# Dividing attention outputs instead of probabilities, and causal scores of two heads in two row tiles

## The reference

```python
# layer 1, full attention with head mixing (head_w sums the six heads' q), then a norm per head
s = q_mixed @ k.T * hd ** -0.5          # 256 x 256 a head
p = softmax(s)
p = (p - mean(p)) / sqrt(var(p) + 1e-5) * gamma + beta      # over the whole 256 x 256 map of a head
y = p @ v
# layers 2 and 3, causal attention
p = softmax(where(causal, q @ k.T * hd ** -0.5, -inf))
y = x + (p @ v) @ w_proj + b_proj
```

## Time and profile before

| | |
|---|---|
| median of 3 runs | 978.55 us (974.76 to 978.98) |
| profiled execution | 974.61 us, of which the span of the trace is 972.6 us |
| busy in the span | PE 83%, DVE 79%, ACT 65%, POOL 20% |
| layer 1 loop | 107 to 329 us |
| causal loop of layer 2 | about 393 to 532 us |
| causal loop of layer 3 | about 655 to 796 us |

### The profile page before, as it was taken

The page is one execution under the profiler, slowest core; times in us unless marked ns, Lnnn a source line. Parts: engine busy times, 40 slices in busy tenths (PEclk is TensorE's granted clock), DMA queues, the critical chain, the costliest instruction groups (busy, mean ns, idle before and its releaser), DMA issues.

```text
span 972.6 us, 19124 instructions
## 1 busy us (share of the span) xinstructions
PE 808.0 (83%) x5550; PEld 630.5 (65%) x5550; DVE 772.7 (79%) x2166; ACT 632.9 (65%) x1931; POOL 192.6 (20%) x234
## 2 busy tenths in 40 slices
PE   0876698889988755899999486559999997999997
PEld 0762576667766653678887356438778877677775
DVE  7327799999999835699999869938999994688886
ACT  0211587777877513689888564248889874688885
POOL 9001423443234110000000000010000010134344
PEclk9997899999999967799999798779999995799999
DMA  5000000000000091466666200035666650313130
GB/s 184 1 0 1 1 1 0 0 0 0 0 0 0 10 121 28 76 93 97 90 87 83 31 1 1 0 62 83 84 97 96 88 75 0 69 41 82 41 82 17
DMA packets 54355, 44.30 MB, mean 46 GB/s; under 512 B 28592, under 2 KB 42544, under 8 KB 54192
## 3 DMA queue, kind: packets, MB, share of 16 engines
q1 hardware_dynamic: 53872, 42.30, 27.9%
q0 software_dynamic: 448, 1.57, 0.6%
HBM read 12.33 MB, written 3.21 MB: 16 GB/s over the span
## 4 chain that ended last, share of the span: by engine, by line
PE 44%; DVE 12%; DMA 3%; issue 1%; ACT 1%; SPq 1%; POOL 0%; POOLq 0%; DVEq 0%; ACTq 0%
PE ps L839 7%; PE ps L850 6%; PE ps L720 6%; PE ps L624 6%; PE ps L670 5%; PE ps L661 3%; PE ps L626 3%; DVE chst L910 2%; DMA qk<-lo 2%; DVE on L929 2%; PE ps L551 1%; PE ps L634 1%; PE ps L635 1%; PE ps L647 1%; PE ps L826 1%
## 5 line engine op out<-in xcount | busy, mean ns | idle before, releaser
L419 ACT ACTIVATE ee<-ps,nmax 128x128 f32<-128x128 f32 (+1 forms) x588 | 249.5, 443 | 11.7 <-DVE nmax L990 9.9
L1031 DVE TENSOR_SCALAR ee<-ee,rrec 128x128 f32<-128x128 f32 (+1 forms) x588 | 174.8, 360 | 5.2
L720 PE MATMUL ps<-w,ee 128*128 128x128 f32 x960 | 137.0, 279 | 19.9 <-DVE ee L1031 19.9
L406 ACT ACTIVATE big<-ps 128x384 f32<-128x384 f32 (+1 forms) x224 | 113.5, 538 | 40.0 <-PE ps L720 39.4
L720 PEld LDWEIGHTS ps<-w,ee 128*128 128x128 f32 x960 | 103.9, 141 | 45.4 <-DVE ee L1031 35.6
L419 ACT ACTIVATION_READ_ACCUMULATOR ee<-ps,nmax 128x1 f32 x588 | 124.2, 211 | 0.0
L990 DVE TENSOR_REDUCE nmax<-ps 128x2 f32<-128x256 f32 x200 | 101.1, 545 | 18.0 <-PE ps L626 18.0
L624 PE MATMUL ps<-qk 128*128 128x128 f32 (+1 forms) x400 | 103.7, 348 | 13.4 <-DMA qk<-lo 10.8
L296 POOL TENSOR_TENSOR big<-qs,w 96x256 f32<-96x256 f32 x108 | 78.8, 761 | 144.4 <-ACT qs L429 144.4
L1234 DVE TENSOR_TENSOR hhl<-ee,hhl 128x512 fp32r<-128x512 f32 x96 | 81.7, 858 | 27.9 <-ACT hhl L525 26.2
L624 PEld LDWEIGHTS ps<-qk 128*128 128x128 f32 x400 | 79.8, 207 | 31.7 <-issue 17.9
(11 more groups left out here) (224 smaller groups left out, 1365.5 us busy)
## 6 DMA issues: line engine op xcount, KB each, us to landing
qk<-hi SPq DMA_DIRECT2D x36, 192.0 KB, 3.7
qk<-hi SPq DMA_DIRECT2D x72, 96.0 KB, 3.8
qk<-lo SPq DMA_DIRECT2D x36, 192.0 KB, 4.8
qk<-lo SPq DMA_DIRECT2D x72, 96.0 KB, 4.6
big<-moe_gate SPq DMA_DIRECT2D x8, 768.0 KB, 6.9
w<-w_in SPq DMA_DIRECT2D x1, 1831.5 KB, 12.9
xc<-x_in SPq DMA_DIRECT2D x4, 384.0 KB, 5.7
l_mix<-on SPq DMA_DIRECT2D x8, 192.0 KB, 6.6
```

The costliest lines, as they stand in the source:

```text
L406: nc.scalar.activation(et[:, h, 0:w], ps[:, 4 + hh, 0:w], ACT.Copy).then_inc(own(l, f"et{hh}"), 1)
L419: last = nc.scalar.activation(ee[:, ke, hh, qc, 0:w], src, ACT.Exp, bias=nmax[:, kp, hh, qc:qc + 1], accum_out=rsum[:, kp, hh, qc:qc + 1])
L720: last = nc.tensor.transpose(ps[:, 4 + hh, b * P:(b + 1) * P], ee[:, u, hh, qc, tc * P:(tc + 1) * P], ident)
L1031: last = V.tensor_scalar(v, v, rrec[:, kp, hh, qc:qc + 1], None, ALU.mult)
```

## The change

Four things, which come together:

1. Probabilities are no longer normalised. `vh` has a one in column 16 of each head's 32, so that `weigh_values` gives the row sums as a 17th output row of each head. `outputs` transposes to tokens by channels in all layers, and the new `normalise_outputs` (DVE) takes the reciprocal of 12 sums a token and multiplies. The row sums of `exps` on ACT go, and so do the reciprocals and the four multiplications of each unit on DVE. `transpose` waits for the exponentials.
2. In layer 1 the sum of squares comes from `bn_stats` of the exponentials (four of 256 columns a unit), put together after the loop by six DVE instructions of 192 or 384 columns.
3. In the causal layers, after `outputs` (moved from u = 1 to u = 0) and `normalise_outputs` (u = 1), the result is transposed back (`outputs_back`, PE, u = 1), copied by ACT (`outputs_by_channel`, first thing in u = 2), multiplied with an unsplit projection (`project_outputs`, PE, u = 2) and added (`add_outputs`, DVE, moved to u = 2). DVE does both `et` copies of u = 1, where ACT did both.
4. The two heads of a causal unit lie in rows 0 to 63 and 64 to 127 of `qk`, so each score matmul uses 64 rows. One mask matmul of 2 x 128 columns a head takes the place of two of 128. `stack` issues twelve DMAs of 48 partitions where it issued six of 96.

Besides, POOL's split of the expert weights (`w1hl`) moves from the end of layer 3 to the end of layer 1.

```diff
-STK = 16 * 6
+STK = 16 * 12
-        qk = sb("qk", [P, 2, NH, 2, N], F32R)
+        qk = sb("qk", [P, 2, NH // 2, 2, N], F32R)
...
                         for t, a0, a1 in moves:
-                            sp.dma_start(qk[t * HD:(t + 1) * HD, par, :, a0:a1, :].bitcast(F32),
-                                         part[:, a0:a1, :].bitcast(F32)).then_inc(own(l, "stacked"), 16)
+                            for hh in range(2):
+                                r0 = hh * 4 * HD + t * HD
+                                sp.dma_start(qk[r0:r0 + HD, par, :, a0:a1, :].bitcast(F32),
+                                             part[hh * (C // 2):(hh + 1) * (C // 2), a0:a1, :].bitcast(F32)).then_inc(own(l, "stacked"), 16)
...
-                    last = nc.scalar.activation(ee[:, ke, hh, qc, 0:w], src, ACT.Exp, bias=nmax[:, kp, hh, qc:qc + 1],
-                                                    accum_out=rsum[:, kp, hh, qc:qc + 1])
+                        last = nc.scalar.activation(ee[:, ke, hh, qc, 0:w], src, ACT.Exp, bias=nmax[:, kp, hh, qc:qc + 1])
...
+            def outputs_by_channel(l, i):
+                act.wait_ge(*upto(l, "oc_ps", i + 2))
+                nc.scalar.activation(oc[0:C, :], ps[0:C, 6, 0:N], ACT.Copy).then_inc(own(l, "oc"), 1)
...
+                        if l > 1 and u == 2:
+                            outputs_by_channel(l, i - 1)
                         exps(l, k + 1, (j + 1) % 2, (u + 1) % 3)
...
-                            h = 2 * u + hh
-                            mm(ps[:, 2 * kp + hh, qc * N:qc * N + w], qk[:, par, h, 0, qc * P:(qc + 1) * P], qk[:, par, h, 1, 0:w],
-                               start=True, stop=False)
-                            last = mm(ps[:, 2 * kp + hh, qc * N + qc * P:qc * N + (qc + 1) * P], identb[:, :], maskb[:, :], start=False, stop=True)
+                            r0 = hh * 4 * HD
+                            mm(ps[:, 2 * kp + hh, qc * N:qc * N + w], qk[r0:r0 + 4 * HD, par, u, 0, qc * P:(qc + 1) * P],
+                               qk[r0:r0 + 4 * HD, par, u, 1, 0:w], start=(qc == 0), stop=False)
+                    for hh in range(2):
+                        diag = ps[:, 2 * kp + hh, :].rearrange("p (b t) -> p b t", t=P)[:, 0::3, :]
+                        last = mm(diag, identb[:, :], mid_dim(maskb[:, :], 1, TPI), start=False, stop=True)
...
+            def outputs_back(l, i):
+                pe.wait_ge(*upto(l, "on", i + 2))
+                for q in range(TPI):
+                    last = nc.tensor.transpose(ps[0:C, 6, q * P:(q + 1) * P], ob[:, q, :], ident)
+                last.then_inc(own(l, "oc_ps"), 1)
+
+            def project_outputs(l, i):
+                pe.wait_ge(*upto(l, "oc", i + 2))
+                for q in range(TPI):
+                    last = mm(ps[:, 6, q * C:(q + 1) * C], oc[0:ONE + 1, q * P:(q + 1) * P], wa(f"l{l}_p", ONE + 1), start=True, stop=True)
                 last.then_inc(own(l, "out_ps"), 1)
...
+                        if l > 1 and u == 2:
+                            project_outputs(l, i - 1)
                         for hh in range(2):
-                            pe.wait_ge(*upto(l, "norm", 2 * k + (hh + 1)))
+                            pe.wait_ge(*upto(l, "exp", 2 * k + (hh + 1)))
...
                         if u == 0:
                             project_qk(l, i + 2, par)
+                            if l > 1:
+                                outputs(l, i - 1)
                         if u == 1:
-                            outputs(l, i - 1)
+                            if l == 1:
+                                outputs(l, i - 1)
+                            else:
+                                outputs_back(l, i - 1)
                             parts_ready(l, i + 2)
                             project_v(l, i + 1, npar)
...
+            def normalise_outputs(l, i):
+                dve.wait_ge(*upto(l, "oq", i + 2))
+                src = ps[:, 6, 0:4 * C].rearrange("p (q h d) -> p q h d", q=TPI, d=2 * HD)
...
+                V.reciprocal(rec, src[:, :, :, HD]).then_inc(own(l, "orec"), 1)
+                dve.wait_ge(*upto(l, "orec", i + 2))
+                for q in range(TPI):
...
+                    last = V.tensor_tensor(dst.rearrange("p (h d) -> p h d", d=HD), src[:, q, :, 0:HD], last_dim(rec[:, q, :], HD), ALU.mult)
+                last.then_inc(own(l, "on" if l > 1 else "added"), 1)
...
                         maxima(l, k + 2, j % 2)
-                        if l > 1 and u != 1:
+                        if l > 1 and u == 2:
+                            add_outputs(l, i - 1)
+                        if l > 1:
                             w = len(blocks(l)) * P
-                            dve.wait_ge(*upto(l, "tr", TR0 + 2 * k + 1))
-                            V.tensor_copy(et[:, 2 * u, 0:w], ps[:, 4, 0:w]).then_inc(own(l, "et0"), 1)
+                            for hh in range(2 if u == 1 else 1):
+                                dve.wait_ge(*upto(l, "tr", TR0 + 2 * k + hh + 1))
+                                V.tensor_copy(et[:, 2 * u + hh, 0:w], ps[:, 4 + hh, 0:w]).then_inc(own(l, f"et{hh}"), 1)
                         if l == 1:
-                            dve.wait_ge(sg("l1_norm"), 2 * k + 2)
-                            dve.wait_ge(sg("l1_ssq"), TR0 + k)
-                            for hh in range(1 if u == 2 else 2):
...
+                            dve.wait_ge(sg("l1_exp"), 2 * k + 2)
+                            for hh in range(2):
+                                for q in range(TPI):
+                                    last = V.bn_stats(est[:, par, q, 2 * u + hh, :], ee[:, u, hh, q, :])
+                            last.then_inc(sg("l1_est"), 1)
...
-                        normalise(l, k + 1, (j + 1) % 2, (u + 1) % 3)
                         if u == 0:
                             keys(l, i + 2)
                         if u == 1:
-                            add_outputs(l, i - 1)
+                            normalise_outputs(l, i - 1)
                             values(l, i + 1, npar)
```

More of the change, by code:

```diff
@@ L143, in hybrid_kernel @@
         junk = sb("junk", [P, N])
[L144 to L146 removed]
+        w1hl = sb("w1hl", [P, 2, NE * HID], F32R)
+        est = sb("est", [P, 2, TPI, NH, 6])
+        esta = sb("esta", [P, B, TPI, NH, 6])
         ssqa = sb("ssqa", [P, B, NH])
@@ L336, in _ @@
                     nc.gpsimd.tensor_tensor(w1hl[:, 1, :], wa("f3_w1"), w1hl[:, 0, :].bitcast(F32), ALU.subtract).then_inc(sg("f3_wlo"), 1)
+                if l == 3:
+                    pool.wait_ge(*upto(l, "et0", START + 3 * B))
+                    pool.wait_ge(*upto(l, "et1", START + 3 * B))
+                    pool.wait_ge(*upto(l, "added", B + 1))
                 if l == 2:
@@ L652, in outputs @@
                 pe.wait_ge(*upto(l, "ot", i + 2))
-                if l == 1:
+                for q in range(TPI):
                     for g in range(2):
-                        for q in range(TPI):
-                            a = (q * 2 + g) * C
-                            last = nc.tensor.transpose(ps[:, 6, a:a + C], ots[0:C, g, q * P:(q + 1) * P], wb("ident", C)[:, 0:C])
-                else:
-                    for t in range(TPI):
-                        for g in range(2):
-                            last = mm(ps[:, 6, t * C:(t + 1) * C], ots[:, g, t * P:(t + 1) * P], wa(f"l{l}_p")[:, g * C:(g + 1) * C],
-                                      start=(g == 0), stop=(g == 1))
+                        a = (q * 2 + g) * C
+                        last = nc.tensor.transpose(ps[:, 6, a:a + C], ots[0:C, g, q * P:(q + 1) * P], wb("ident", C)[:, 0:C])
+                last.then_inc(own(l, "oq"), 1)
+            def outputs_back(l, i):
[7 more added lines that the diff above has]
+                    last = mm(ps[:, 6, q * C:(q + 1) * C], oc[0:ONE + 1, q * P:(q + 1) * P], wa(f"l{l}_p", ONE + 1), start=True, stop=True)
                 last.then_inc(own(l, "out_ps"), 1)
@@ L736, in _ @@
                 outputs(l, B - 1)
+                if l > 1:
+                    outputs_back(l, B - 1)
+                    project_outputs(l, B - 1)
                 pe.wait_ge(*upto(l, "max", 3 * B + 2))
@@ L1010, in add_outputs @@
             def add_outputs(l, i):
                 dve.wait_ge(*upto(l, "out_ps", i + 2))
-                if l == 1:
-                    for q in range(TPI):
-                        src = ps[:, 6, q * 2 * C:(q + 1) * 2 * C].rearrange("p (h d) -> p h d", d=2 * HD)[:, :, 0:HD]
-                        dst = on1[:, q, i + 1, :] if isinstance(i, int) else on1[:, q, bass.ds(i + 1, 1), :].rearrange("p a c -> p (a c)")
-                        last = V.tensor_copy(dst.rearrange("p (h d) -> p h d", d=HD), src)
-                else:
-                    tv = tok_all[:, bass.ds(i * TPI + TPI, TPI), :]
-                    last = V.tensor_tensor(tv, ps[:, 6, 0:TPI * C].rearrange("p (t c) -> p t c", c=C), tv, ALU.add)
@@ L1021, in add_outputs @@
-                last.then_inc(own(l, "added"), 1)
```

(26 more changed lines are left out.)

94 lines of the change are left out of this document (53 added, 41 removed).

## The result

The changed kernel takes **1116.5 us** (median of 4 runs, 1114.6 to 1119.6) against 978.0 for the kernel before in the same comparison: ratio 1.143, 95% interval 1.139 to 1.147. It is slower by 138 us. The forecast was 1073, with a range of 1022 to 1118, so the time lies at the range's upper edge, 43.5 us above the forecast. The stop of PE that the forecast rests on is there, and a second cost, that of the clock, was sized far too small.

A forecast was written before the change was run, and what follows sets the result against it. Layer 1 was taken as bound by PE with DVE close behind, the causal layers by PE's own work. 974.6 - 22 + 3 + 99 + 3 + 14 = 1071.6, forecast 1073 us, range 1022 to 1118.

The forecast's parts named there:

- Layer 1, -22: Layer 1's loop: PE's waits for DVE's normalisation go, 19.9 us, and a little more as weight loads run ahead.
- End of layer 1, +3: After layer 1's loop: six added DVE instructions in a chain, about 3 us in plain view.
- The stop at `ob`, 2.5 us an image: Causal loops, u = 1: PE stands still at `outputs_back` until DVE has normalised the outputs, 2.5 us an image.
- The round, 11.75 us and +99: Causal loops: the outputs' way between engines makes an image 11.75 us against 8.64, +99 us over 32 images.
- Rival 1: Causal scores: changing the array's tiles costs, S 1.23 us instead of 0.86, 1109 us; chance 0.14 together with rival 2.
- The clock, +14: Causal loops: half clock behind PE's stop, up to 51 us if in each image; a fourth to a third taken.
- Ends of layers, +3: End of each causal layer: normalisation, transposes back, ACT's copy and three hand-overs add 1.5 us, 3 in all.
- The DMAs, a floor of 9.3 to 11.8 us under cover of the round: Causal loops: `hi`, eleven issues and the last landing take 9.3 to 11.8 us an image, barely covered by the round.
- Rival 5: Causal loops: the issue chain binds beyond the round, 12.4 us an image, 1094 us; chance 0.07.
- Rival 3: Causal scores: heads overlap, S 0.43 us, no loss of clock, 1018 us; chance 0.12 with what lies between 985 and 1040.
- Rival 2: Causal loops: the clock falls in every image, 1073 + 37 = 1110 us; chance 0.14 together with rival 1.
- Rival 4: Causal loops: no stop of PE at `outputs_back`, PE's work bounds at 7.5 us an image, 923 us; chance of faster 0.06.

The follow-up runs named there:

- Experiment 11: Kernel before with layer 1's part of the change alone, the 32 token-sum matmuls moved ahead of the one that waits for `ssqa`: 952.7 us, ratio 0.974.
- experiment 4: Changed kernel with 20 matmuls whose result nobody reads ahead of `outputs_back`, during PE's stop: 1037.8 us, ratio 1.060.
- experiments 5 and 6: Changed kernel with both heads' scores from partitions 0 to 63 (5: 1103.4 us), or with each scores matmul over all 128 partitions (6: 1070.5 us).
- experiments 7 and 8: Changed kernel with `normalise_outputs` ahead of the maxima in u = 1 (7: 996.2 us), and `add_outputs` ahead of them in u = 2 too (8: 996.8 us).
- experiment 10: Changed kernel with normalisation and addition of outputs ahead of the maxima, and two of twelve `qk` DMAs issued by ACT's queue: 969.1 us, ratio 0.992.
- the four kernels: Changed kernel (1116.5 us), and it with one row tile (1103.4), all rows (1070.5), or the scores, masks and six DMAs of before (1072.8).

## Why the prediction came out as it did

- **Layer 1, -22:** right in mechanism, the loop gave 27.9 (by its first and last maxima). PE bound with DVE covered, as said. The waits of 19.9 us went, and the image shrank by 1.7 us instead of 1.25 (0.89 + 0.36). The further 0.4 us was called "a little more" and not broken down; no run isolates it.
- **End of layer 1, +3:** too small, 7.5 measured. The three microseconds of added DVE chain were right (300.92 to 304.0). What was left out is that PE's 32 matmuls stood behind it in the queue, and then ran at half clock, 3.3 us more. Experiment 11 shows that part: moved ahead, they run at full clock.
- **The stop at `ob`, 2.5 us an image:** right, 2.3 us by PE's rows, with each instruction of DVE in the order forecast; DVE's part is shorter than summed, 2.53 us from the maxima to `ob` (506.32 to 508.85) for 2.85.
- **The round, 11.75 us and +99:** the chain was right, some terms in it too long; 11.05 was measured at full clock (experiment 4). Scores were taken at 0.86 us a unit, from the middle of 0.43 and 1.23; they took 0.65. But only two of the three units count, 0.42 us: in u = 1 the maxima wait for DVE's own `lo`, the branch that the prediction had coming to the same place at the same time (`lo` from 505.71 to 506.40, when PE was already at T). DVE's part, above, is another 0.32. The round cost 2.35 us an image, and 74 us over the two loops, not 99. Rival 1's mechanism is there, but smaller than its price: by experiments 5 and 6 the change to 64 rows costs 0.14 us and the 64-row unit 0.11 more, and the overlap gives back 0.23. The Trainium skill, "TensorEngine Tiling (Array Packing)", Key Properties, speaks of a drain at such a change; these rows agree with it.
- **The clock, +14:** this is the step that failed. "If it falls in each image, the 1.6 us of PE work behind the stop take up to twice as long, 51 us", and a fourth to a third of that was taken. It stayed at half for 6.8 of 13.65 us, and a mean of 0.74 and 0.77 over the loops is what that gives in nearly every image (1 less half of 6.8 / 13.65 is 0.75). Those 6.8 us are transposes back, values, scores, projection, T, the weighing and part of the next scores. Measured: 13.65 - 11.05 = 2.6 us an image, 72 us over the two loops of after and experiment 4, 79 by their whole times. Both mistakes have one root: the cost of a fall was taken as that of the next few instructions, while the earlier trace rows already showed 0.51 from 3 to 5 us after the idle time had ended; and the fall was expected in a fourth to a third of the images and came in nearly all.
- **The sum:** the two errors in the loops, 25 us too much for the round and 58 too little for the clock, partly cancel, and this is luck: it is why the time still lies in the range. The loops grew by 147 us for a forecast 113, layer 1 with its end gave 18 for 19, everything else grew by 12 for 3. One of the prediction's own signs says the same: with the clock under 0.9 in the causal loops it was to be wrong upward.
- **Ends of layers, +3:** 6.6 between the loops and 4.7 behind layer 3. In experiment 4 the loops are 3.2 us further apart than before, so half of the 6.6 came with the clock; no run takes the rest apart.
- **The DMAs, a floor of 9.3 to 11.8 us under cover of the round:** right. The floor is 9.68, in the changed kernel it is covered (PE and ACT waited for `qk` three times each in the whole program), and it came up as the bound as soon as the stop went (experiments 7 and 8). Rival 5 didn't occur, since the landing fell to 2.1 us.
- **Rival 3** (1018, the heads overlap and nothing else adds) has its first half right, with half of the gain, and the second wrong. **Rival 2** (the clock falls in every image) is the one that occurred; its price was 51 us for 72, and its 1110 lies near the time because the round in it was 25 us too long. **Rival 4** (faster) asked for two things, no stop at `outputs_back` and DMA issues of under 0.5 us. Neither is quite reached: an issue stays at 0.6 us, and in experiment 10 a stop of 0.44 us is left. But with the stop cut and two issues moved to ACT, and with layer 1's gain, the whole change comes below the kernel before, 969.1 us.

**What stays open.** Why the clock is kept in more images with all rows than with row tiles after the same stop: the four kernels show that it is so, not whether the form of the scores does it or the length of the image, which sets where the stops lie in time. And in experiment 10 the causal image is 8.84 us against 8.70 before: PE still waits there 0.44 us for `ob`. The causal half of the change was nowhere seen to pay by itself: with it at its best the time is 969.1, without it 955.5.

## What to carry to other kernels

Follow a new round trip between engines instruction by instruction in the order of the queues: here one call that stood behind three others on DVE was worth 120 us, and both its effects, the wait and the clock behind it, went with it. Price a stop of PE by how long the clock stays at half behind it (6.8 us here), not by the instructions next to it. When two chains are nearly as long as each other, expect nothing from shortening one. Before DMAs are split, multiply the count by the issue time (0.63 us here) and set it against the length of the loop.
